# A reciprocal on VectorE replaced by logarithm and exponential on ScalarE with one Newton step, in a two-layer kernel

## What is computed

```python
k = k_in @ Wk
v = v_in @ Wv
r = jax.nn.sigmoid(r_in @ Wr)

def step(carry, kv):
    num, den, mx = carry
    ck, cv = kv
    max_out = jnp.maximum(mx, ck + tf)
    e1 = jnp.exp(mx - max_out)
    e2 = jnp.exp(ck + tf - max_out)
    out = (e1 * num + e2 * cv) / (e1 * den + e2)
    ...

return r * rwkv @ Wo
```

## Time and profile before

| | us |
|---|---|
| median of 3 runs | 487.36 (486.51 to 487.36) |
| the profiled execution | 488.38 |
| its span, first to last instruction | 486.60 |
| TensorE busy in the span | 426.3 (88%) |
| VectorE busy | 328.0 (67%) |
| ScalarE busy | 189.9 (39%) |
| mean granted clock | 0.962 |

### The profile page before, as it was taken

The page is one execution under the profiler, slowest core; times in us unless marked ns, Lnnn a source line. Parts: engine busy times, 40 slices in busy tenths (PEclk is TensorE's granted clock), DMA queues, the critical chain, the costliest instruction groups (busy, mean ns, idle before and its releaser), DMA issues.

```text
span 486.6 us, 4142 instructions
## 1 busy us (share of the span) xinstructions
PE 426.3 (88%) x1392; PEld 207.3 (43%) x1392; DVE 328.0 (67%) x663; ACT 189.9 (39%) x307; POOL 20.5 (4%) x35
## 2 busy tenths in 40 slices
PE   4963898799979959999999999999999999999942
PEld 2331565566825435344544444335534333342310
DVE  4999898799646953596988685574636842642543
ACT  1342757533154311445234355252056535325211
POOL 0010211100000000000000000000000000000000
PEclk9996998989999979999999999999999999999977
DMA  6300000120000000000000000000000000000000
GB/s 231 118 1 1 1 0 1 41 100 1 0 2 2 0 0 1 0 1 0 2 0 0 1 5 16 2 0 0 0 1 0 24 0 1 0 0 1 0 22 22
DMA packets 5152, 7.27 MB, mean 15 GB/s; under 512 B 1080, under 2 KB 4236, under 8 KB 4876
## 3 DMA queue, kind: packets, MB, share of 16 engines
q1 hardware_dynamic: 3972, 4.80, 2.9%
q10 hardware_dynamic: 1160, 2.21, 1.2%
HBM read 5.95 MB, written 1.05 MB: 14 GB/s over the span
## 4 chain that ended last, share of the span: by engine, by line
PE 53%; DVE 8%; issue 5%; ACT 4%; POOLq 0%; POOL 0%; DVEq 0%; ACTq 0%
PE ring L1199 19%; PE ring L1178 7%; PE specbank L253 4%; PE ring L1194 4%; PE ring L1180 4%; PE ring L1207 2%; PE timebank L265 2%; PE ring L1220 2%; PE ring L1224 1%; PE ring L1221 1%; PE timebank L274 1%; DVE hm L1385 1%; PE ring L1213 1%; PE ring L1190 1%; PE ring L1215 1%
## 5 line engine op out<-in xcount | busy, mean ns | idle before, releaser
L1199 PE MATMUL ring<-hm,wc 128*128 128x512 f32 x240 | 108.3, 601 | 0.0
L1199 PEld LDWEIGHTS ring<-hm,wc 128*128 128x128 f32 x240 | 44.0, 190 | 63.0 <-issue 55.5
L197 PE MATMUL bankA<-wconv,h2w 128*128 128x256 f32 x128 | 34.0, 412 | 5.1 <-ACT h2w L568 5.1
L1385 DVE SCALAR_TENSOR_TENSOR hm<-xtm,cst,h 128x512 f32<-128x512 bf16 x48 | 33.3, 746 | 7.4 <-ACT h L1300 7.4
L1313 ACT ACTIVATE gts<-ring 128x512 f32<-128x512 f32 x16 | 9.6, 597 | 52.7 <-PE ring L1199 52.7
L1300 ACT ACTIVATE h<-ring,vec 128x512 f32<-128x512 f32 x32 | 21.9, 687 | 18.1 <-PE ring L1180 15.7
L197 PEld LDWEIGHTS bankA<-wconv,h2w 128*128 128x128 f32 x128 | 24.7, 203 | 9.5 <-ACT h2w L568 5.8
L1458 DVE SCALAR_TENSOR_TENSOR f2e<-hl,f2e 128x512 f32<-128x512 f32 x8 | 5.5, 691 | 32.9 <-ACT hl L1341 32.9
L1194 PE MATMUL ring<-hm,wc 64*128 64x512 f32 x80 | 22.6, 641 | 0.3 <-DVE hm L1385 0.3
L265 PE MATMUL timebank<-cst,abc 128*128 128x256 f32 x96 | 22.6, 394 | 0.0
L1213 PE MATMUL ring<-xn,wc 128*128 128x512 f32 x16 | 10.8, 762 | 12.8 <-DVE xn L1453 12.6
(11 more groups left out here) (256 smaller groups left out, 754.9 us busy)
## 6 DMA issues: line engine op xcount, KB each, us to landing
wc<-in_w_c SPq DMA_DIRECT2D x1, 1664.0 KB, 7.0
cst<-in_const ACTq DMA_DIRECT2D x1, 1096.0 KB
out<-xall SPq DMA_DIRECT2D x8, 128.0 KB, 1.9
wc<-in_x_feat SPq DMA_DIRECT2D x1, 768.0 KB, 12.1
bconv<-in_bcast SPq DMA_DIRECT2D x1, 512.0 KB, 6.6
wc<-in_k_time ACTq DMA_DIRECT2D x1, 512.0 KB
wc<-in_x_feat ACTq DMA_DIRECT2D x1, 256.0 KB, 3.6
wa<-in_w_a SPq DMA_DIRECT2D x1, 256.0 KB, 3.5
```

The costliest lines, as they stand in the source:

```text
L197: pe.matmul(at, h2w[:, n, h * P + tap:h * P + tap + P], wconv[:, tap, :], start=(tap == 0), stop=False)
L1199: ins = pe.matmul(dst[:, :], wc[:, at:at + P], hm[:, seat(j, made + g - 1), :], start=False, stop=(g == PAIRS - 1))
L1385: dve.scalar_tensor_tensor(hm[:, seat(j, k), :], picked, cst[:, C_EG + g:C_EG + g + 1], h[:, g, :], ALU.is_equal, ALU.mult).then_inc(S["hm ...
```

## The change

The reciprocal is made as exp(-ln d). ScalarE takes the logarithm of the denominator, scaled by 2 to the -30, and then the exponential of minus that with a bias that takes the scale out again; the result is the tile `guess`. VectorE refines it by one Newton step: for a denominator d and a guess g it computes (d g - 2) g, which is minus the refined reciprocal. The sign is taken back by multiplying Wo by -0.5 where it was 0.5. VectorE's instruction at 814 is gone, and two instructions (832, 833 in the new numbering) are added per chunk. A small Ln (579) stands ahead of `xbf`, as the small Exp stands ahead of the exponentials. `conv_weights()` moves from behind `output_end(0)` to before it. GpSimd sets one more constant.

```diff
+                    if valid(c):
+                        act.activation(der[:, DEXP:DEXP + 1], der[:, DTOP:DTOP + 1], ACT.Ln)
                     if valid(c - 1):
                         act.wait_ge(x1_turned, c)
 
                         act.activation(xbf[:, :], pst[:, :], ACT.Copy).then_inc(xbf_ready, 1)
                         act.wait_ge(xbf_ready, c)
                         act.activation(q32[:, :], xbf[:, :], ACT.Identity, scale=der[:, DRI:DRI + 1]).then_inc(xs_ready, 1)
+                    if valid(c):
+                        act.wait_ge(den_ready, c + 1)
+                        act.activation(guess[:, :], dn[:, :], ACT.Ln, scale=DEN_SCALE).then_inc(den_log, 1)
+                        act.wait_ge(den_log, c + 1)
+                        act.activation(guess[:, :], guess[:, :], ACT.Exp, scale=-1.0, bias=der[:, DLOG:DLOG + 1]).then_inc(guess_ready, 1)
                     pieces(c - 2, (0,))
...
-                dve.tensor_scalar(wa[:, W_O:W_O + P], wa[:, W_O:W_O + P], 0.5, None, ALU.mult).then_inc(weights_mixed, 1)
+                dve.tensor_scalar(wa[:, W_O:W_O + P], wa[:, W_O:W_O + P], -0.5, None, ALU.mult).then_inc(weights_mixed, 1)
...
-                    rec.go(dve.tensor_tensor(pair(dn[:, :]), pair(expo[:, 2, :]), prev(den, c), ALU.add))
+                    dve.tensor_tensor(pair(dn[:, :]), pair(expo[:, 2, :]), prev(den, c), ALU.add).then_inc(den_ready, 1)
                     rec.link(dve.tensor_tensor(ta[:, :], expo[:, 2, :], vsb[:, :], ALU.mult))
-                    rec.go(dve.reciprocal(dn[:, :], dn[:, :]))
                     rec.go(dve.tensor_tensor(pair(ta[:, :]), pair(ta[:, :]), prev(num, c), ALU.add))
 
                 def output_end(c):
                     rec.wait()
+                    dve.wait_ge(guess_ready, c + 1)
+                    rec.link(dve.tensor_tensor(dn[:, :], dn[:, :], guess[:, :], ALU.mult))
+                    rec.link(dve.scalar_tensor_tensor(dn[:, :], dn[:, :], -2.0, guess[:, :], ALU.add, ALU.mult))
                     rec.link(dve.scalar_tensor_tensor(dn[:, :], thr[:, :], 1.0, dn[:, :], ALU.add, ALU.mult))
...
                         output(c)
+                        conv_weights()
                         output_end(c)
-                        conv_weights()
```

More of the change, by code:

```diff
@@ L58 @@
 RATIO_TOP = 60.0
+DEN_SCALE = 2.0 ** -30
 LN2 = float(np.log(2.0))
@@ L376, in two_layers @@
             k8 = sb("k8", [P, P], BF16, st)
-            der = sb("der", [P, 9], F32, st)
-            DTD, DOM, DRI, DRK, DSS, DTOP, DEXP = 0, 1, 4, 5, 6, 7, 8
+            der = sb("der", [P, 10], F32, st)
+            DTD, DOM, DRI, DRK, DSS, DTOP, DEXP, DLOG = 0, 1, 4, 5, 6, 7, 8, 9
             rowf = sb("rowf", [3, R_ALL], F32, st)
@@ L392, in two_layers @@
             thr = sb("thr", [P, TOK], F32, st)
+            guess = sb("guess", [P, TOK], F32, st)
             expo = sb("expo", [P, 3, TOK], F32, st)
@@ L453, in two_layers @@
             scans_done = sem("scans_done")
+            den_ready = sem("den_ready")
+            den_log = sem("den_log")
+            guess_ready = sem("guess_ready")
             rwkv_ready = sem("rwkv_ready")
@@ L714, in _ @@
                 pool.memset(der[:, DTOP:DTOP + 1], RATIO_TOP)
+                pool.memset(der[:, DLOG:DLOG + 1], float(np.log(DEN_SCALE)))
                 pool.memset(mx[:, :, 0:1], -1e38)
```

## The result

The changed kernel takes **489.09 us** (median of 20 runs, 486.81 to 490.69), the kernel before 487.30 over its 20 runs: ratio 1.0039, interval 1.0027 to 1.0050. It is some 0.4% slower, where 0.6% faster was forecast. The forecast range ended at 486.6.

What follows compares the result with a forecast made beforehand. The first stage's ring of VectorE, TensorE and ScalarE was taken to bound, its end set by chunk 2's norm. Running gains of 1.5, 2.3, 2.2 and 2.8 us through chunks 0 to 3 gave 487.36 - 2.8 = 484.5, range 482.0 to 486.6.

Steps and rivals of the forecast that it cites:

- moves as a whole: Second stage, behind the barrier: TensorE's, 316 of 348 us busy; it only shifts with the first stage's end.
- the longer low stretch of body 4: Gap before body 4 grows by 1.4 us, which can cost up to 0.9 by a longer low-clock stretch.
- the likeliest case: The forecast itself: the whole kernel 2 to 3.7 us faster, chance 0.60.
- has nothing to do: Chunk 0: ScalarE is free at the denominator, VectorE waits 0.35 us for the guess; chunk 1's maxima start 1.5 us earlier.
- A fourth term, in chunk 3: Chunk 3: rounding starts 4.3 us earlier; less 1.44 for two steps, the norm of chunk 2 is 2.8 us earlier.
- Chunk 1: VectorE waits 1.1 us for `q32`, the guess ties; `xq` 3.7 us earlier, `y2b` 2.3 earlier.
- Chunks 2 and 3: VectorE waits for `q32`, 3.3 us in chunk 2, about 2 in chunk 3; gains stand at 2.2, then 2.8 us.
- the norm of chunk 2: Starts TensorE's last run of the first stage through `xall`; forecast 2.8 us earlier, and the barrier with it.
- The clock gives more back: Rival: shorter TensorE gaps in the first stage return the full clock sooner; 481.5 to 483.5 us, chance 0.20.
- The round trip is longer than its cover: Rival: extra switch or Ln time shows in every chunk; 492.5 us at 1.28 us more per switch; slower, chance 0.07.
- e = 0.2: Every chunk: 0.2 us more per table switch, about 5 to 6 e lost by the end; gain said still 2.1 us.
- It does not get rid of the wait: Rival: each guess comes 1.8 us late, so waiting replaces the reciprocal: 487.4 us; little or nothing left, chance 0.13.

Runs made afterwards that it cites:

- the second trace of after: The changed kernel, unchanged, timed and traced a second time: 488.60 us, ratio 1.0026 to the kernel before.
- the variant with the guess first: Changed kernel with ScalarE making chunk 0's guess ahead of copying chunk 1's key: 488.04 us; with two filling products before the barrier 485.10 us.
- the first timing: The changed kernel's first 20 runs against the kernel before: 489.09 us, ratio 1.0039.
- all five of the changed order: Unfilled: changed kernel twice (489.09, 488.60 us), and with guess ahead of key copy (488.04), x_feat transfer earlier (487.92), or convolution weights back in place (489.29).

## Why the prediction was wrong

Three steps failed. By size they are that the second stage "moves as a whole" (+1.5 us instead of 0), that the longer low stretch of body 4 was left out of the likeliest case (+1.0), and that ScalarE "has nothing to do" in chunk 0 (about 1 us of gain that did not come). A fourth term, in chunk 3, was half a microsecond too large. Together they make the 3.95 us between the forecast of -2.8 and the +1.15 that the traces give on average.

**Chunk 0: wrong.** The step that failed is "ScalarE has nothing to do then". It was read from the idle time of the kernel before, and not from what stands ahead in ScalarE's order. The copy of chunk 1's key projection does, it had waited for TensorE before as well, and TensorE waited for `x_feat`. Before, nobody wanted ScalarE meanwhile; now the guess does. VectorE waited 2.87 us, not 0.35. How late the copy is depends on the clock of the projection as well: in the second trace of after, at the full clock, the wait was nothing, and chunk 0 went as forecast, with the maxima at 26.65 (forecast 26.9). Putting the guess first gave about 1 us. The first milestone moved by 0.55 us on average instead of 1.5.

**Chunk 1: right.** The waits are 0.93 us for `q32` (forecast 1.1) and none for the guess (a tie); the stretch to `y2b` is 0.92 shorter, forecast 0.8. A load takes 1.28 us and Ln 0.61, nearer to the lower bound of 0.60 than to the 0.72 taken.

**Chunks 2 and 3: the mechanism was right, a term too large.** VectorE waits 3.18 and 2.82 us for `q32` (forecast 3.3, and in chunk 3 about 2). The output got no shorter there, as said. But the stretch to `y2b` of chunk 3 shrank by 0.1 instead of 0.6. `q32` of chunk 3 ended 15.8 us after that `y2b` of chunk 2 in the trace of after and 16.8 in that of before, 1.0 less where the forecast had 1.5. TensorE computes at the low clock on the way to it, before as after (and the row at 77.12 with 3.40 us for a piece that takes 1.99), so this alone does not explain the half microsecond; two traces of one kernel differ by as much at `y2b` of chunk 2.

**Up to the norm of chunk 2** the gain is thus 1.35 us on average (0.55 and 0.8), not 2.8.

**Body 4: a rival in the forecast, undervalued.** It said that the longer gap "can cost up to 0.9 by a longer low stretch", and left that out of the likeliest case. The low stretch doubled, and `xall` to the barrier takes 1.0 us more on average. TensorE had to wait 2.39 us for `xall` there, against 0.94 before, so the gap grew as forecast.

**"The second stage moves as a whole": wrong.** This was not priced at all. TensorE is idle for 2.80 us ahead of the second stage, no longer than the 2.81 before, but now the clock stays low for 6.8 us behind the barrier, where it did for 0 and 3.4 us, and the stage takes 1.5 us more on average. Three products there took 1.9 us off the changed kernel, and two took 2.9 off the variant with the guess first.

**The sum.** -1.35, +1.0 and +1.5 make +1.15; the spans of the two pairs of traces say +1.3 and +1.0. The medians say +1.8 in the first timing and +1.3 in the second. What of the first is left, 0.6 us, is not located: traces are single executions, and the start alone differs by 1.9 us.

**The rivals.** "The clock gives more back" had the right mechanism with the wrong sign. In chunk 1 the low stretch did get shorter with the gap, from 10.2 us in both plain traces of before to 6.8 in both of after, but the transform began sooner too, and the clock came back 3.9 and 4.8 us after its start, where it had been 4.8 and 3.6. It took 5.52 and 5.99 us, against 5.96 and 5.44: nothing gained. Elsewhere the clock cost more. Filled by hand, the gap of body 1 was worth 2.7 us, within the 1 to 3 that this rival named, though 0.9 of it came in body 4. "The round trip is longer than its cover" fell: the rows 23.01, 23.64 and 24.94 stand 0.02 us apart. The trace of after, too, shows nothing of the drain that the prediction cites from the Trainium skill, ScalarE: Activation LUTs, section What ACT_TABLE_LOAD costs. (In that rival the 2.1 us left at e = 0.2 do not follow from its own 5 to 6 e, which leave 1.6 to 1.8; nothing hangs on it.) "It does not get rid of the wait" came true in chunk 0 alone, and in three of the four traces.

**Open.** Why the low stretches became longer with the changed order isn't shown. The runs show that they did, in every unfilled kernel of that order, and that a few products in the gap take them away, in most places. At the barrier TensorE's gap is as long before as after, so a longer gap is not the cause there.

## What to carry to other kernels

A wait that you read as free time on an in-order engine belongs to the instruction behind it: before you put urgent work there, look at what stands ahead, and what that hangs on. Taking work off one engine moves the gaps of the others and lengthens some of them. Where that other is TensorE, each gap is to be priced with the rows that come after it at the low clock, also behind a barrier, where the code has not changed. A cheap test tells the two apart: fill the gaps with a few products in both kernels, and compare these. Then look at the granted clock of both traces, since a filled kernel can have a low stretch in a new place, as before did here, and the difference is then not the change alone.

## What the runs showed of the hardware

- The same eight-matmul product took 1.99 us at the full clock, 3.78 where the clock was granted at half throughout, and 3.40 where it fell 0.3 us after the start. I had expected gaps to cost their own length; here two products at the end of a stage gained 2.9 us in a kernel of 488.
- The low stretch behind one and the same wait is not the same every time: behind the barrier, after 2.8 us of idle time on TensorE, it lasted 0 and 3.4 us in the two plain traces of before and 6.8 in all five of the changed order.
- Extra products in TensorE's gaps cost little: ten of them in before left it 0.9 us faster, eleven in after 7.5 us faster. Two at the end of the stage made before 0.6 us slower.
- A load of ScalarE's table starts 0.02 us behind the activation before it and costs 1.28 us, also between Ln and Exp, so that Ln, load and Exp of a 128x512 tile take 2.65 us in a row.
- One transfer issued one place earlier was worth 1.2 us: the projection that waited for `x_feat` to 17.18 and 17.02 in the two traces of after began at 13.50. The other thing that made it late was the clock: at nearly the same start its first pair of products took 2.07 us in one trace and 1.13 in the other.
